# Graph attention over a sparse adjacency: the last two half tiles signed in parts, the last rank between two rows of mixing, sums over slots by three additions

## The reference

```python
h = jnp.maximum(_layernorm(x, axis=-1), 0.0)
s_i = h @ attn[:d]
s_j = h @ attn[d:]
e = leaky_relu(s_i + s_j.T, negative_slope=0.2)
e = e + jnp.where(adj > 0, 0.0, -1e9)
out = x + softmax(e, axis=1) @ h
```

## Time and profile before

| | |
|---|---|
| median of 3 runs | 806.81 us (806.52 to 807.26) |
| profiled execution | 807.28 us, of which the span is 805.5 us |
| VectorE busy | 629.0 us (78%) |
| ScalarE busy | 534.2 us (66%) |
| GpSimd busy | 530.7 us (66%) |
| TensorE busy | 359.0 us (45%) |
| loads of adj | 277.04 MB with the other loads and stores of that queue |

### The profile page before, as it was taken

One profiled execution on the slowest core, in us unless ns is written; L12 is line 12 of the kernel. 1 busy time (PEld: TensorE's weight loads), 2 busy tenths in 40 slices (PEclk: granted clock), 3 DMA queues, 4 the chain that ended last, 5 costly groups with the idle time before them and its releaser, 6 DMA issues.

```text
span 805.5 us, 6460 instructions
## 1 busy us (share of the span) xinstructions
PE 359.0 (45%) x1361; PEld 162.0 (20%) x1380; DVE 629.0 (78%) x2112; ACT 534.2 (66%) x413; POOL 530.7 (66%) x526
## 2 busy tenths in 40 slices
PE   0454433344443434344444434344443634755663
PEld 0231111111111111111111111111110311633463
DVE  6898379787668667789768676789769899999773
ACT  4995676766666666667667666766766667675550
POOL 6630677755557777756557777756557776777674
PEclk9875756555555555555555555555555555877576
DMA  8999999999999999999999999999999999994120
GB/s 341 397 404 433 391 405 407 409 408 410 412 412 408 409 410 407 407 413 413 412 412 407 408 411 407 406 413 415 413 415 407 408 409 408 405 406 141 44 58 9
DMA packets 39864, 300.23 MB, mean 373 GB/s; under 512 B 10768, under 2 KB 17544, under 8 KB 22288
## 3 DMA queue, kind: packets, MB, share of 16 engines
q1 hardware_dynamic: 24176, 277.04, 84.7%
q0 software_dynamic: 15360, 22.51, 8.1%
q10 hardware_dynamic: 288, 0.26, 0.1%
HBM read 303.76 MB, written 8.98 MB: 388 GB/s over the span
## 4 chain that ended last, share of the span: by engine, by line
DMA 74%; issue 12%; DVE 5%; ACT 5%; PE 2%; POOL 1%; SPq 0%; POOLq 0%; DVEq 0%; ACTq 0%
DMA adj_ring<-in_adj_dram 74%; ACT sign_ring L658 3%; ACT h_all L670 2%; DVE one_hot L774 1%; PE words L1562 1%; ACT sign_ring L651 0%; DVE sums L1075 0%; PE words L1522 0%; POOL out_dram L596 0%; DVE cand L819 0%; DVE terms L1070 0%; PE words L1579 0%; POOLq L101 0%; PE words L1687 0%; PE words L1558 0%
## 5 line engine op out<-in xcount | busy, mean ns | idle before, releaser
L658 ACT ACTIVATE sign_ring<-adj_ring,half_neg 128x4096 fp8e3<-128x4096 int32 x127 | 471.2, 3710 | 210.1 <-DMA adj_ring<-in_adj_dram 206.0
L555 POOL DMA_INDIRECT near<-h_table,near_id x384 | 415.7, 1083 | 208.3 <-issue 117.4
L1522 PE MATMUL words<-sign_ring,pack_w 128*128 128x512 bf16 x511 | 219.0, 578 | 357.2 <-ACT sign_ring L658 355.9
L819 DVE MAX8 cand<-words 128x8 f32<-128x256 f32 x256 | 90.8, 416 | 96.4 <-PE words L1522 96.4
L1522 PEld LDWEIGHTS words<-sign_ring,pack_w 128*128 128x128 bf16 x512 | 53.6, 124 | 518.8 <-ACT sign_ring L658 449.0
L1075 DVE TENSOR_REDUCE sums<-terms 128x128 f32<-128x1024 f32 x58 | 111.8, 1927 | 2.0
L566 POOL DMA_INDIRECT near_m<-h_table,id_m x64 | 65.5, 1023 | 19.9 <-issue 18.9
L1070 DVE TENSOR_TENSOR terms<-near,weight 128x512 f32<-128x512 f32 (+1 forms) x87 | 72.2, 855 | 0.0
L1511 PE MATMUL words<-place,place_w 128*128 128x512 bf16 x110 | 54.9, 583 | 7.3 <-DVE key L982 3.9
L1548 PEld LDWEIGHTS listing<-cand,one_hot 128*128 128x128 f32 x128 | 32.6, 312 | 11.5 <-issue 7.2
L1501 PE MATMUL listing<-h_all 128*1 128x128 f32 x128 | 18.5, 316 | 26.4 <-ACT h_all L670 26.4
(11 more groups left out here) (296 smaller groups left out, 531.4 us busy)
## 6 DMA issues: line engine op xcount, KB each, us to landing
adj_ring<-in_adj_dram SPq DMA_DIRECT2D x127, 2048.0 KB, 24.5
near<-h_table,near_id POOLq DMA_INDIRECT x384, 6.4
h_table<-h_all POOLq DMA_DIRECT2D x4, 1056.0 KB, 14.7
x_all<-in_x_dram SPq DMA_DIRECT2D x4, 1024.0 KB, 9.3
out_dram<-x_all SPq DMA_DIRECT2D x30, 128.0 KB, 23.7
adj_ring<-in_adj_dram SPq DMA_DIRECT2D x2, 1024.0 KB, 25.9
near_m<-h_table,id_m POOLq DMA_INDIRECT x64, 6.4
out_dram<-x_all ACTq DMA_DIRECT2D x2, 128.0 KB, 1.8
```

Of the source, the lines that this page charges most:

```text
L555: pool.indirect_dma_start(out=near[:, p % RING, k, :], out_offset=None, in_=table, in_offset=bass.IndirectOffsetOnAxis(ap=near_id[:, p % I ...
L658: nc.scalar.activation(bytes_of, adj_ring[:, n % HALVES, :].rearrange("p (d r i) -> p d r i", r=2, i=WORDS), ACT.Sign, bias=half_neg[:, :] ...
L819: last = nc.vector.max(out=cand[:, p % 2, t % 2, 8 * q:8 * q + 8], in_=words[t % 3][:, q * PART:(q + 1) * PART])
L1522: last = nc.tensor.matmul(at[:, k * BANK:(k + 1) * BANK], pack_w[:, d, :], twins[:, o + k * BANK:o + (k + 1) * BANK], start=False, stop=(d ...
```

## The change

Half 126 is loaded and signed in two parts as half 127 is; the second parts have two semaphores and two columns of the degree. TensorE mixes row 0 of pair 29, ranks pair 31, then mixes row 1. The reduction over the eight slots is replaced by three additions that halve the number of slots, so a pair's steps in the semaphore `mixing` go from 8 to 12. `lone_end(LAST)` moves from behind the eleventh to behind the thirteenth step of `add_deep`.

```diff
-        MIX = 8
+        MIX = 12
-        LAST_HALF = 2 * TILES - 1
-        LONE_BETWEEN = 11
+        PARTED = 2 * TILES - 2
+        LONE_BETWEEN = 13
...
-                    if n == LAST_HALF:
-                        sp.dma_start(adj_ring[:, n % HALVES, 0:HALF // 2], adj_t[n // 2, :, HALF:HALF + HALF // 2]) \
-                            .then_inc(adj_in[n % HALVES], 16)
-                        sp.dma_start(adj_ring[:, n % HALVES, HALF // 2:HALF], adj_t[n // 2, :, HALF + HALF // 2:N]) \
-                            .then_inc(last_in, 16)
+                    if n >= PARTED:
+                        for d in range(2):
+                            at = slice(d * HALF // 2, (d + 1) * HALF // 2)
+                            cols = slice(n % 2 * HALF + d * HALF // 2, n % 2 * HALF + (d + 1) * HALF // 2)
+                            sp.dma_start(adj_ring[:, n % HALVES, at], adj_t[n // 2, :, cols]) \
+                                .then_inc((adj_in[n % HALVES], last_in[n - PARTED])[d], 16)
...
-                    if n == LAST_HALF:
+                    if n >= PARTED:
                         for d in range(2):
                             at = slice(d * HALF // 2, (d + 1) * HALF // 2)
                             if d == 1:
-                                act.wait_ge(last_in, 16)
+                                act.wait_ge(last_in[n - PARTED], 16)
...
-                nc.vector.tensor_reduce(sums[:, a, :], terms[:, :, :].rearrange("p k d -> p d k"),
-                                        AX.X, ALU.add).then_inc(mixing, 1)
+                nc.vector.tensor_tensor(terms[:, 0:4, :], terms[:, 0:4, :], terms[:, 4:8, :], ALU.add) \
+                    .then_inc(mixing, 1)
                 dve.wait_ge(mixing, m + len(runs) + 1)
+                nc.vector.tensor_tensor(terms[:, 0:2, :], terms[:, 0:2, :], terms[:, 2:4, :], ALU.add) \
+                    .then_inc(mixing, 1)
+                dve.wait_ge(mixing, m + len(runs) + 2)
+                nc.vector.tensor_tensor(sums[:, a, :], terms[:, 0, :], terms[:, 1, :], ALU.add).then_inc(mixing, 1)
+                dve.wait_ge(mixing, m + len(runs) + 3)
...
-            dve.wait_ge(first_signed, 1)
-            nc.vector.tensor_tensor(degree[:, TILES - 1, 1:2], degree[:, TILES - 1, 1:2], last_degree[:, :], ALU.add) \
+            dve.wait_ge(first_signed, 2)
+            nc.vector.tensor_tensor(degree[:, TILES - 1, :], degree[:, TILES - 1, :], last_degree[:, :], ALU.add) \
...
-                    if n == LAST_HALF and d == DIGITS // 2:
-                        pe.wait_ge(first_signed, 1)
-                    elif n == LAST_HALF or d % (DIGITS // 2) == 0:
+                    if n >= PARTED and d % (DIGITS // 2) == 0:
+                        pe.wait_ge(first_signed, n - PARTED + 1)
+                    elif n >= PARTED or d % (DIGITS // 2) == 0:
...
-                for a in range(2):
+                for a in rows:
...
-            mix_pair(BODY)
+            mix_pair(BODY, (0,))
             rank_pair(PAIRS - 1)
+            mix_pair(BODY, (1,))
```

More of the change, by code:

```diff
@@ L159, in graph_attention_kernel @@
         degree = sb("degree", [P, TILES, 2], fp32)
-        last_degree = sb("last_degree", [P, 1], fp32)
+        last_degree = sb("last_degree", [P, 2], fp32)
         fullest = sb("fullest", [P, 2], fp32)
@@ L319, in graph_attention_kernel @@
         signed = sem("signed")
-        last_in = sem("last_in")
+        last_in = [sem(f"last_in{i}") for i in range(2)]
         first_signed = sem("first_signed")
@@ L653, in sign_tile @@
                                                  ACT.Sign, bias=half_neg[:, :], saturate=False,
-                                                 accum_out=(degree[:, t, h:h + 1], last_degree[:, :])[d]) \
+                                                 accum_out=(degree[:, t, h:h + 1], last_degree[:, h:h + 1])[d]) \
                                 .then_inc((first_signed, signed)[d], 1)
@@ L1055, in add_row @@
             def add_row(g, a):
-                m = MIX * g + 2 + 3 * a
+                m = MIX * g + 2 + 5 * a
                 e = g % RING
@@ L1550, in list_pair, with mix_pair @@
                 last.then_inc(listed, 1)
-            def mix_pair(g):
+            def mix_pair(g, rows=(0, 1)):
                 i = g - BODY
@@ L1563, in mix_pair @@
                                                 start=False, stop=(k == own - 1))
-                last.then_inc(closing_ready, 1)
+                if rows[-1] == 1:
+                    last.then_inc(closing_ready, 1)
             def lone_ranks(b):
```

## The result

The changed kernel takes **810.0 us** (median of 6 runs, 809.53 to 810.61) where the kernel before took 806.68 on the same chip (6 runs, 805.59 to 807.26): ratio 1.0041, 95% interval 1.003 to 1.0051, so 3.3 us slower. Forecast were 805.5 us and a range from 804.3 to 807.2. The profiled execution took 810.15 us for a span of 808.4; the span before was 805.5.

The account below looks back on a forecast made before the run. Loads of adj bound the kernel, so only time behind the last load can be won. Parts give 0.27 us, additions 0, the earlier rank most; through the last store 1.3 gained: 805.5 us against the median, range 804.3 to 807.2.

Parts of the forecast that it names:

- the landing of the last byte stays: Last loads: half 126 in parts starts the last sign 0.27 us earlier, its whole yield; the last landing does not move.
- So 0 on the path; what is late in its place is the load: VectorE's reduction: three additions take 1.4 for 1.93 us a row, 30 us saved over the kernel, nothing on the path.
- GpSimd's cover: GpSimd before pair 31's gathers: 3.37 us to spare absorbs a fall-back near 1.5; cost 0, or 0.6 if it breaks.
- if the tree moves the pace of the loads at all: Sign of being wrong: the three additions (the tree) change the pace of the loads, forecast not to change.
- The rank between the rows: TensorE's tail: ranking pair 31 between pair 29's rows brings VectorE's key 2.6 us earlier, 2.8 with the 0.27; find 2.1 earlier.
- the score's new wait: VectorE's score of the deep list would wait for the last deep gather, which it did not before, starting 1.03 us earlier.
- 1.3 us gained: End of the kernel: GpSimd's last store starts at 796.65 against 797.94; 1.0 to 1.6 by that store alone.
- the rival of the eaten gain: GpSimd's train meets about 1 us more stretch, or last loads land half a microsecond later: 0.2 gained or nothing, 806.7; 15%.
- The windows by which the prediction lets each row grow: VectorE's additions: windows grow about 1.4 us a row, which one gather may meet, at 0 to 1.0 us.
- The slower rival: VectorE's two-input instructions hold up GpSimd's 25 gathers from 755.85 on: up to 2.7 us lost, 809.5; chance 9%.
- the signs of being wrong: Last part landing over 0.7 off 747.8, GpSimd busy at 755.5, score starting at loop end, or the tree moving the loads' pace.

Follow-up runs that it names:

- e11: Kernel before with 32 halves (48 to 79) each loaded as two column parts, signed whole: 872.73 us, ratio 1.0825 to the kernel before.
- e13: Kernel before with halves 122 to 126 each loaded as two column parts, signed whole: 812.9 us, ratio 1.0116 to the kernel before.
- e8: The kernel before itself, unchanged, run again for a profile: 804.42 us, ratio 1.0001 to the kernel before.
- e17: Whole change, but the three additions only for pairs 0 to 23, the reduction for the others: 806.38 us, ratio 1.0027 to the kernel before.
- e18: Whole change, but the three additions only for pairs 24 to 28, the reduction for the others: 803.88 us, ratio 1.0001 to the kernel before.
- e5: The whole change again, on a second chip: 806.67 us, ratio 1.0028 to the kernel before.
- e6: Half 126 in parts and the three additions, without the rank between the rows: 806.94 us, ratio 1.0027 to the kernel before.
- e9: The whole change again, on a third chip: 810.99 us, ratio 1.0049 to the kernel before.
- e10: Whole change plus twelve matmuls that nothing reads, in TensorE's idle time ahead of half 125's words: 809.42 us, ratio 1.0042 to the kernel before.
- e3: Only the rank of pair 31 between the rows of pair 29's mix, put into the kernel before: 804.21 us, ratio 0.9999.
- e12: Kernel before with 32 halves (48 to 79) each loaded as two transfers of 64 partitions: 967.3 us, beside 806.25 for the kernel before.

## Why the prediction was wrong

*"the landing of the last byte stays"* (half 126 in parts, cost 0): **this step failed.** A half in two transfers costs 2.1 us in the body (e11) and 1.9 at the end (e13); the last sign came 1.5 us later in the mean of the table's second column, 2.4 in the two profiles of the section on the result. I read the slices of the earlier trace rows, saw the engines over 90% busy, and took the bytes as what counts. But the rate at which busy engines move bytes was not constant: 410 GB/s at a share of 1.01 in e8, 293 at 0.99 in e11. The profile had the sign of it: the earlier trace rows has half 127's own parts travelling 24.7 and 27.1 us, for 1 MB each, while whole halves of 2 MB take 24.5 in the median; and from 725 to 730 us, with these parts in flight, its engines moved 290 GB/s at a busy share of 1.01.

Nor is the mean rate what ends the last load. In the kernel before, from 735 to 745 us, the DMA engines are busy for a share of 0.19 and move 51 GB/s, while half 126 (which lands at 742.4) and both parts of 127 are still out; in the kernel after it is 0.22. That the last landing hangs on the few engines that are furthest behind is argued from these shares; the traces don't tell the engines apart.

*"So 0 on the path; what is late in its place is the load"* (the additions): the sizes were right, 1.41 a row, and GpSimd's cover held (it comes to pair 31 2.5 us later than before, at 754.69, and still waits 4.53). That *they* make the load later was what I had named as proof of an error ("if the tree moves the pace of the loads at all"), and it does: 1.0 to 1.5 us between halves 112 and 122, and e17 and e18 pin it to the additions before 628 us. They had ended by the stretch that is longer, so it is not their own traffic that holds up a load; it is the order of the work, which they leave shifted. What in it stays open. The mean rate in the stretch is the same (405 to 410 GB/s), so more moves in it (23.1 to 23.4 MB for 22.8 to 23.0), nearly all of it adj: the half was overtaken rather than the engines slowed. Whether by the one gather more into `near` that GpSimd issues there in most of these kernels (29 for 27 or 28) was not tried.

*Why either alone shows nothing.* In the second run of the kernel before (e8) VectorE's last maxima do not wait for TensorE, where the earlier trace rows has a wait of 0.34:

```profile
748.54 1.42 DVE L819 MAX8 cand<-words 128x8 f32<-128x256 f32 x4
```

Pair 31's second gathers then follow the last sign by 8.6, not by the 7.8 to 7.9 that stand where the load is the last to come. So the old VectorE chain hides 0.7 to 1.2 us of a late load in such runs. 1.2 for the additions or 1.5 for the parts, less this, is within what an interval of ±0.1% can miss; the two together, 2.7 less 0.7, make 2.0, near the 2.3 and 2.2 of e5 and e6. The 3.3 and 4.0 of the first comparison and of e9 have longer second stretches (33.4, 33.3); the lower clock explains little of it, since e10, without it, stays at 1.0042. This sum is argued from the table; no run takes the slack away by itself.

*The rank between the rows*: right in its links up to the deep gathers and in the score's new wait, and worth nothing: e3 is at 0.9999. The term that failed is the "1.3 us gained". 0.36 of it was an idle time that the one profile had, and e8 hasn't: there the deep gathers start 10.42 behind pair 31's second gathers without a wait, as they do with the change (10.41). Another 0.6 went to the rival of the eaten gain, at its place and for over half of its price of 1: VectorE's products come earlier against GpSimd's train, and the gather that starts with the first of them takes 1.89 for 1.32. So the score, forecast 1.03 earlier, came no earlier against those gathers. The end stands 49.0 to 49.2 behind them with the rank moved, and 48.4 (e8) to 49.7 without.

The gather's stretch follows a pattern that the earlier trace rows had: it ended 0.88 after the product's end there, and ends 0.87 after it here (774.83 + 1.89 against 774.63 + 1.22). They start 0.1 and 0.2 into the product. The gather of 774.41 in the earlier trace rows started 0.76 into the product of the kernel before (773.65, 1.22 long), took 1.32 and ended 0.86 after it. So in these three a gather's loss is set by how early in the product it starts. With GpSimd's cover intact these stretches did not make the loss.

The windows by which the prediction lets each row grow, 1.4 us in which the additions hold a gather at 0 to 1.0, were my estimate from the product of the earlier trace rows, and no run shows them at this size. In the kernel after, the 54 gathers that start inside an addition of 512 or 256 take 0.99 to 1.03, and the 61 that started inside a reduction took 0.99 to 1.01. Inside a product of 1024 a gather takes 2.00 in the median in both kernels; inside one of 512, with an addition behind it, it takes 1.16, where it took 1.00 with the reduction behind.

*The slower rival* had another mechanism and place (the train from 755.85 on, up to 2.7 lost). Its stretches came, 0.8 more than before, but to the end 0.5 was won there, not lost. The 3.3 us slower are not its doing, and no rival held the cause that the runs show; only the signs of being wrong named the last landing and the pace of the loads.

## What to carry to other kernels

Where loads bound a kernel, don't take the split of a transfer as free: price it by putting it on many transfers in the middle of the kernel (e11), where 2 us each become 66, before judging it on one at the end. A step that is free alone can cost together with another one, when both spend the same slack; test the pair, and one of them by its place. And don't count as gain an idle time that one profile has: a second profile of the same kernel (e8) would have shown that over a quarter of the forecast gain wasn't there.

## What the runs showed of the hardware

- Two transfers of 64 partitions by 16 KB moved at 223 GB/s, two of 128 partitions by 8 KB at 293, one of 128 by 16 KB at 410, at busy shares of the DMA engines of 1.02, 0.99 and 1.01 (e12, e11 and e8, from 300 to 400 us). With the halves of the partitions in transfers of their own the rate fell by 46%, with the halves of the columns by 29%.
- The rows of one half lie 2 MB apart in memory (64 rows of 32 KB between neighbouring partitions), and whole halves run from there into SBUF at 410 GB/s (e8). Whether the pitch is what slows the split ones, no run here shows.
- A load's last bytes trail the rest: from 735 to 745 us in the kernel before, the engines' busy share is 0.19, at 51 GB/s, with three loads still to land.
- TensorE's four packing matmuls of half 125 took 1.89 us at a granted clock of 0.50 in the kernel after and in e9, where it had idled 4.85 and 4.32 us behind the lone matmuls. With twelve more matmuls in that gap (e10) they took 1.04 at 1.00.
